# Scan pass of a two-layer image model: rows by channel then state, replicated in a quarter of the transfers; gathered rows squared in thirds; compare marks in 8 bits; a ring of six tie masks

## What is computed

```python
sim = jnp.einsum('bdl,bd->bl', xn, cn)
sort_idx = jnp.argsort(-sim, axis=1)
inv_idx = jnp.argsort(sort_idx, axis=1)
xseq = jnp.take_along_axis(x_conv.reshape(b, D, L), sort_idx[:, None, :], axis=2)
xs = jnp.stack([xseq, jnp.flip(xseq, -1)], axis=1)
...
def step(hst, t):
    dt_l, B_l, C_l, x_l = t
    dA = jnp.exp(dt_l[..., None] * A)
    hst = dA * hst + (dt_l * x_l)[..., None] * B_l[:, :, None, :]
    y = jnp.einsum('bkdn,bkn->bkd', hst, C_l)
    return (hst, y)
...
y = jnp.take_along_axis(y, inv_idx[:, None, :], axis=2).reshape(b, D, h, w)
yl = jnp.transpose(y, (0, 2, 3, 1))
mu = jnp.mean(yl, -1, keepdims=True)
var = jnp.var(yl, -1, keepdims=True)
yl = (yl - mu) / jnp.sqrt(var + 1e-05) * norm_gamma + norm_beta
```

## Time and profile before

| | |
|---|---|
| median of three runs | 18248.87 us |
| the profiled execution | 18395.5 us |
| its span, first to last instruction | 18392.4 us |
| a lap of pass one, mean of ten | 307.9 us |
| pass one | about the first 10300 us of the span |
| PE, DVE, ACT, POOL busy, of the span | 72%, 77%, 48%, 67% |
| mean granted TensorE clock | 0.826 of full speed |

### The profile page before, as it was taken

How to read it: one execution, slowest core, us unless ns; L and a number is a source line. 1 busy time by engine, 2 the same in 40 slices (tenths; PEclk the granted TensorE clock), 3 DMA queues, 4 the chain that set the end, 5 groups by cost and what they waited for, 6 DMA issues and landing times. The chain is left out here.

```text
span 18392.4 us, 187064 instructions
## 1 busy us (share of the span) xinstructions
PE 13268.3 (72%) x52714; PEld 6518.8 (35%) x53295; DVE 14108.2 (77%) x18932; ACT 8908.6 (48%) x16476; POOL 12335.6 (67%) x10756
## 2 busy tenths in 40 slices
PE   6777777777777777777776366666666666666665
PEld 3333333333334333433332133333333333333332
DVE  4788888888878888888877277777777777777777
ACT  4556565655555555555554244444444444444442
POOL 3777777777777777777777266666666666666665
PEclk8899999999999999999988577777777777777776
DMA  2333333333333333333333355555555555555554
GB/s 53 96 99 99 98 99 97 101 96 100 96 95 101 97 101 97 101 97 100 98 95 94 88 159 160 158 157 157 154 159 159 158 160 160 161 158 155 158 159 130
DMA packets 1297950, 2235.15 MB, mean 122 GB/s; under 512 B 713341, under 2 KB 759125, under 8 KB 1284629
## 3 DMA queue, kind: packets, MB, share of 16 engines
q1 hardware_dynamic: 896022, 1090.20, 22.8%
q0 software_dynamic: 368640, 1076.24, 20.6%
q10 hardware_dynamic: 32256, 56.64, 1.0%
HBM read 1493.27 MB, written 275.76 MB: 96 GB/s over the span
## 5 line engine op out<-in xcount | busy, mean ns | idle before, releaser
L1608 POOL DMA_INDIRECT G<-corners,idx x5184 | 4929.0, 951 | 3260.6 <-issue 1407.9
L1368 POOL TENSOR_TENSOR hc<-h,crep 128x768 f32<-128x768 f32 x2304 | 4177.3, 1815 | 2245.5 <-DVE h L1165 1086.8
L1149 DVE TENSOR_TENSOR ps<-dxr,ps 128x768 f32<-128x768 f32 x2304 | 2192.2, 951 | 1274.4 <-PE ps L752 1103.9
L1165 DVE TENSOR_TENSOR_SCAN h<-decay,carry,ps 128x768 f32<-128x768 f32 x1536 | 2777.0, 1808 | 90.6 <-ACT decay L986 37.5
L763 PE MATMUL ps<-hc,sel 128*96 128x512 f32 (+1 forms) x6144 | 2431.7, 521 | 474.9 <-POOL hc L1368 362.7
L986 ACT ACTIVATE decay<-dtr,a_neg 128x768 f32<-128x768 f32 x2304 | 2121.5, 927 | 522.3 <-DVE h L1165 504.4
L1897 DVE TENSOR_TENSOR G<-G,ps 128x1152 f32<-128x1152 f32 (+1 forms) x1152 | 1724.8, 1497 | 0.0
L1639 PE MATMUL ps<-cols_t,w_def 128*96 128x384 f32 x3456 | 1443.5, 583 | 316.2 <-ACT prow L1827 298.9
L752 PE MATMUL ps<-bq,pick 128*128 128x256 bf16 (+1 forms) x4027 | 1083.8, 342 | 795.3 <-DVE h L1165 496.2
L763 PEld LDWEIGHTS ps<-hc,sel 128*96 128x96 f32 x6144 | 972.7, 174 | 1678.5 <-issue 1058.8
L883 PE MATMUL ps<-xcp,w_local 128*96 128x384 f32 x3456 | 1459.0, 544 | 130.3 <-ACT local_c L1054 130.3
(11 more groups left out here) (235 smaller groups left out, 24443.8 us busy)
## 6 DMA issues: line engine op xcount, KB each, us to landing
crep<-c_rows SPq DMA_DIRECT2D x3072, 96.0 KB
dtr<-rel SPq DMA_DIRECT2D x2304, 96.0 KB
dxr<-one_e SPq DMA_DIRECT2D x2304, 96.0 KB
corners<-prow SPq DMA_DIRECT2D x1536, 72.0 KB
G<-corners,idx POOLq DMA_INDIRECT x5184
x_in<-in_x SPq DMA_DIRECT2D x32, 864.0 KB
local_all<-local_c ACTq DMA_DIRECT2D x192, 144.0 KB
sim<-sorted_rows SPq DMA_DIRECT2D x32, 864.0 KB, 6.8
```

The lines of the kernel that those rows point to most:

```text
L1149: dve.tensor_tensor(drive, dxr[:, q % 2, cg, :], drive, ALU.mult).then_inc(S["s_drive"], 1)
L1165: dve.tensor_tensor_scan(along(h[:, v % HR, :], k), along(decay[:, v % 3, :], k), along(wide(bank_of("step", v % STEPS), P), k), first, AL ...
L1368: pool.tensor_tensor(hc[:, v % HC, :], h[:, v % HR, :], crep[:, g % CRING, :], ALU.mult).then_inc(S["s_weighted"], 1)
L1608: pool.indirect_dma_start(M["G"][:, slot(g), k, :], None, table(r), bass.IndirectOffsetOnAxis(M["idx"][side(r)][:, t, k:k + 1], 0)).then_i ...
```

## The change

1. **Rows by channel, then state.** Row `p` of the 128 becomes channel `p // 4` of state `p % 4`. The constants `pick` and `sel` and the load of `a_log` follow; so a replication is one transfer to 128 rows whose source repeats each row four times, three instead of 12 for `dtr` and for `dxr`, one instead of four for `crep`. All bytes are moved as before.
2. **Gathered rows squared in thirds.** ACT squares six tiles each in steps 13, 16 and 19, each tile with an accumulated sum, and waits only for the six gathers that it needs (a semaphore for each third). DVE's sum of the squares goes; the roots are made in steps 20 and 21, the scaling in 22 to 24.
3. **Comparisons** start at step 17 instead of 19, in 8 bits; the tie masks start at 16, a step ahead of the comparisons, in a ring of six.
4. `HC` is six. The normalisation starts at step 38 instead of 40, and a chunk's nine taps are spread over four steps (3, 2, 2, 2) from step 44. The first round's state inputs come in step 4 instead of 3.

```diff
-    state = np.repeat(np.arange(N).reshape(NG, NG), GS, axis=1)
+    state = np.tile(np.arange(N).reshape(NG, NG), (1, GS))
...
-    c["sel"] = (np.arange(P)[:, None, None] % GS + GS * np.arange(CG)[None, :, None] == r[None, None, :]).astype(
+    c["sel"] = (np.arange(P)[:, None, None] // NG + GS * np.arange(CG)[None, :, None] == r[None, None, :]).astype(
...
-HC = 5
+HC = 6
...
-E_NORM = 17
+E_SQUARE = (13, 16, 19)
+E_NORM = 20
...
-O_CMP = 19
+O_CMP = 17
+O_TIE = O_CMP - 1
+TIES = 6
...
-NORM = 40
+NORM = 38
 CONV = NORM + 6
+CONV_TAPS = (0, 3, 5, 7, TAPS)
+CPARTS = len(CONV_TAPS) - 1
...
-BC_AT = (3, 16, 27, 38, 51, 63)
+BC_AT = (4, 16, 27, 38, 51, 63)
...
                 for g in range(CG):
-                    for j in range(NG):
-                        sp.dma_start(rep[j * GS:(j + 1) * GS, q % 2, g, :],
-                                     src[g * GS:(g + 1) * GS, :]).then_inc(S[f"{done}{g}"], 16)
+                    sp.dma_start(rep[:, q % 2, g, :], src[g * GS:(g + 1) * GS, :].unsqueeze(1).to_broadcast([GS, NG, SC])
+                                 ).then_inc(S[f"{done}{g}"], 16)
...
-                for j in range(NG):
-                    n = NG * (g % NG) + j
-                    sp.dma_start(crep[j * GS:(j + 1) * GS, g % CRING, :],
-                                 dram["c"][q % 2, n:n + 1, :].partition_broadcast(GS)).then_inc(S[f"s_crep{g % CRING}"], 16)
+                n = NG * (g % NG)
+                sp.dma_start(crep[:, g % CRING, :], dram["c"][q % 2, n:n + NG, :].unsqueeze(0).to_broadcast([GS, NG, SC])
+                             ).then_inc(S[f"s_crep{g % CRING}"], 16)
...
-                    for t in range(3 * part, 3 * part + 3):
+                    for t in range(CONV_TAPS[part], CONV_TAPS[part + 1]):
...
+                if s in E_SQUARE:
+                    i = E_SQUARE.index(s)
+                    act.wait_ge(S[f"e_gather{i}"], (lap[0] + 1) * each_gather)
...
+                    for t in range(TPS * i, TPS * (i + 1)):
+                        m = act.activation(M["e_squares"][:, t % TPS, :], ended[:, t, :], ACT.Square,
+                                           accum_out=M["var_y"][:, t:t + 1])
+                    m.then_inc(S["e_sq"], 1)
                 n = s - E_NORM
                 if n == 0:
-                    act.wait_ge(S["e_gather"], past("e_gather") + 16 * NT)
...
-                    act.activation(e_squares, ended[:], ACT.Square).then_inc(S["e_sq"], 1)
...
                 if n == 1:
-                    dve.wait_ge(S["e_sq"], past("e_sq") + 1)
-                    dve.tensor_reduce(var_y[:], e_squares, AX.X, ALU.add).then_inc(S["e_var"], 1)
-                if n == 3:
...
-                t, _ = sub_chunk(s, O_CMP, 1, NT)
+                t, _ = sub_chunk(s, O_TIE, 1, NT)
...
-                    if t >= 2:
-                        pool.wait_ge(S["o_ranked"], past("o_ranked") + t - 1)
+                    if t >= TIES:
+                        pool.wait_ge(S["o_ranked"], past("o_ranked") + t - TIES + 1)
```

More of the change, by code:

```diff
@@ L272, in build_program @@
                      "s_added", "s_y", "s_yturned", "s_yrows", "s_ystored",
[L273 to L274 removed]
+                     *[f"e_gather{i}" for i in range(NSC)], "e_sq", "e_root", "e_inv", "e_norm", "e_back", "e_out", "e_saved0", "e_saved1")
+            dma = [S["o_scatter"], *[S[f"e_gather{i}"] for i in range(NSC)]]
             own = [s for s in S.values() if s not in dma]
@@ L476, in pass_one_memory @@
         tall=tall, x=low("x_in", [L]), xn=b("xnp", [P, PH, PW]), xpad=low("xcp", [PH, PW]), sim=b("sim", [P, L]),
-        rows=b("rows", [P, NT, C]), unit=b("unit", [P, NT, C]), cmp=b("cmp", [P, 2, L], BF16),
-        tie=b("tie", [P, 2, P], BF16), same=b("same", [P, P]), one=b("one", [P, 1], BF16), work=low("work", [3, CH]), local=b("local_c", [C, 2, CH]),
+        rows=b("rows", [P, NT, C]), unit=b("unit", [P, NT, C]), cmp=b("cmp", [P, 2, L], FP8),
+        tie=b("tie", [P, TIES, P], BF16), same=b("same", [P, P]), one=b("one", [P, 1], BF16),
+        one8=b("one8", [P, 1], FP8), e_squares=b("e_squares", [P, NT // NSC, C], BF16), work=low("work", [3, CH]), local=b("local_c", [C, 2, CH]),
         zpart=b("zpart", [C, NCH]), rlen=b("rlen", [P, NT]), root_x=b("root_x", [P, NT]), dist=b("dist", [P, NT]),
@@ L513, in pass_one, with gathered @@
     dtr, dxr, crep, decay, h, hc = (M[n] for n in ("dtr", "dxr", "crep", "decay", "h", "hc"))
+    each_gather = 16 * NT // NSC
+    def gathered(eng, laps_done):
+        for i in range(NSC):
+            eng.wait_ge(S[f"e_gather{i}"], laps_done * each_gather)
     chunk = lambda c: slice(c * CH, (c + 1) * CH)
@@ L650, in store_rows @@
                 if E and i == 1:
-                    sp.wait_ge(S["e_gather"], past("e_gather") + 16 * NT)
+                    gathered(sp, lap[0] + 1)
                 tiles = slice(TPS * c, TPS * (c + 1))
@@ L1019, in normalise @@
                     act.activation(newton, inv, ACT.Square).then_inc(S["n_inv"], 1)
-                c, part = sub_chunk(s, CONV, 3)
-                if c is not None and part == 2:
+                c, part = sub_chunk(s, CONV, CPARTS)
+                if c is not None and part == CPARTS - 1:
                     act.wait_ge(S["n_conv"], past("n_conv") + c + 1)
@@ L1075, in end @@
                     act.activation(M["sq_y"][:], M["inv_y"][:], ACT.Square).then_inc(S["e_root"], 1)
-                if 4 <= n < 4 + NSC:
+                if 2 <= n < 2 + NSC:
                     act.wait_ge(S["e_inv"], past("e_inv") + 1)
-                    for t in range(TPS * (n - 4), TPS * (n - 3)):
+                    for t in range(TPS * (n - 2), TPS * (n - 1)):
                         m = act.activation(ended[:, t, :], ended[:, t, :], ACT.Copy, scale=M["root_y"][:, t:t + 1])
@@ L1224, in order @@
                     if j == 0 and E:
-                        dve.wait_ge(S["e_gather"], past("e_gather") + 16 * NT)
+                        gathered(dve, lap[0] + 1)
                     if j == 0 and lap[0]:
@@ L1333, in ties @@
                     pool.wait_ge(S["o_same"], past("o_same") + t + 1)
-                    pool.tensor_tensor(M["tie"][:, t % 2, :], M["same"][:], Wt["before"][:],
+                    pool.tensor_tensor(M["tie"][:, t % TIES, :], M["same"][:], Wt["before"][:],
                                        ALU.mult).then_inc(S["o_tie"], 1)
             def pad(s):
-                c, part = sub_chunk(s, CONV + 3, 3)
+                c, part = sub_chunk(s, CONV + CPARTS, CPARTS)
                 if c is not None and part == 0:
@@ L1384, in _ @@
             if E:
-                pool.wait_ge(S["e_gather"], laps * 16 * NT)
+                gathered(pool, laps)
             if O:
```

50 lines of the change are left out of this document (24 added, 26 removed).

## The result

| | before | after |
|---|---|---|
| median of four runs | 18250.65 us | 18093.13 us |
| the profiled execution, and its span | 18395.5, 18392.4 us | 18102.84, 18101.0 us |
| ten laps of pass one | 3079.0 us | 3017.0 us |

The ratio is 0.991, with an interval of 0.9894 to 0.9926. The change is faster by about 160 us, where 579 were forecast and the range ended at 240. The two profiled executions stand 292.7 us apart, more than the medians; of that, 131 us lie behind the last lap, in pass two, which the change does not touch. So I go by laps, 6.2 us shorter in these ten instead of 18.7.

A forecast was written before the change was run, and what follows sets the result against it. A pass-one lap is DVE's work plus its idle time, with POOL or DVE full by stretch. 8.2 - 1 + 1 + 4 + 5.5 + 1 = 18.7 us a lap, 579 in all, gave 17670 us (17400 to 18010).

The forecast's parts named there:

- The first state inputs in step 4: Moving them puts 1.6 us of POOL's work behind the first `rel`, in the same stretch: forecast to cost nothing.
- Spreads: Merged `dtr` and `dxr` transfers: gains of 1 us a lap at the first `dxr` and 4 in the fifth round.
- The issues shrink from 7.6 to 1.9 us, less 1.1 for data: Fifth round, ACT's wait for `dxr` before overwriting `one_e`: 4.6 of 5.64 us saved, taken as 4 (1 to 4.8).
- the term of 1 us: DVE's 3.7 us wait for the first `dxr` ends, but POOL bounds that stretch: 1 us a lap (0 to 3.7).
- Squares: DVE's sum and the wait before it go: 8.2 us a lap, not less than 4; ACT's price loses 1 (0 to 5).
- Masks: Masks made two POOL steps ahead of PE's use shorten DVE's waits for `replicate`: 5.5 us a lap (1 to 8).
- Taps: Same 54 taps a lap over 24 steps instead of 18, with HC and normalisation: gain of 1 us (-2 to 3).
- Eight bits: 8-bit comparison results on DVE, and PE's products with them: no time gained, only memory.
- POOL eats it: Rival, 0.17: DVE runs into POOL's products in both full stretches; 267 us gained, 17980; sign: PE's wait well above 11.6 us.
- The data, not the issues: Rival, 0.10: data set the spreads' length, so both spread terms vanish; 13.7 us a lap, 422 us gained, 17825.
- a merged transfer goes to so few DMA engines that it ends slower: Rival, 0.05: on four of 16 engines, third group 10 us late in each of six rounds; 19700 us.

The follow-up runs named there:

- the three moves: Changed kernel with comparisons at step 19 (masks at 18), first state inputs in step 3 and squares in steps 15, 17, 19: 0.9798 of the kernel before.
- the kernel of the squares: Kernel before with only the squares in thirds and 8-bit comparisons: 0.9916; with its comparisons and masks at step 17 instead of 19: 0.997.

## Why the prediction was wrong

**The account.** Worked out from ratios: squares 153 us, masks 97 to 119, spreads 55 to 62, taps 0; against it the state inputs in step 4, 66, and the comparisons at 17, 88 to 99. The sum lies between 140 and 180, and 157 to 172 were measured; such a sum takes it that the parts do not act on each other. The squares' steps do not appear in it: their cost shows only once the inputs are moved.

**The step that failed most** is "The first state inputs in step 4 ... nothing, the same work lies in the same stretch", together with the comparisons' start, for which my sum has no term at all. I counted work and not places, and POOL's work alone. PE's work is the same, but two insertions in one step leave no step between them and the `replicate`, and the bank that it needs is emptied behind the other insertion. The order of instructions showed both; I did not follow who frees the bank. In the same way the comparisons' two steps cost no instruction, yet they move the comparisons, their masks and POOL's scatters against a softplus and step sizes that stay where they were, and in steps 33 and 34 a `replicate` then stands behind a late mask. Together these are 154 to 165 us of the 420 that are missing; of the rest some 97 are the spreads (155 less 58), 63 the squares (216 less 153), 62 the masks (170 less 108) and 30 the taps. (My sum for the last lap, 8.2, left out the spreads and ACT's loss, which it has too: 12.2, a slip of 4 us.)

**Spreads**: the step "The issues shrink from 7.6 to 1.9 us, less 1.1 for data". The mechanism was right and the size wrong. SP's queue in the fifth round of the lap, and the wait that it ends, against the earlier trace rows:

```profile
3846.29 3.81 SPq L631 DMA_DIRECT2D dtr<-rel  x3
3850.14 5.70 SPq L631 DMA_DIRECT2D dxr<-one_e  x3
```

```profile
L948 ACT ACTIVATE one_e<-mag,ones 96x768 f32<-96x768 f32 x60 | 56.1, 935 | 48.8 <-DMA dxr<-one_e 47.2
```

Three transfers hold SP for 3.8 to 5.7 us, not 1.9. I had set the data of one group (1.5 us) against the issues of three; three groups are 1.18 MB, by my own 258 GB/s 4.6 us. (That the third transfer cannot be issued before the first has drained, as I put it for a later run, is not what the trace shows: the third `dtr` was issued by 3850.1, and the first landed at 3851.8.) The wait of ACT fell from 5.86 us a lap (58.6 in the ten laps of before) to 4.72, DVE's behind it from 4.27 to 2.44. The first `dxr` was in time in after, but that was luck. With the state inputs in step 4, POOL's `remainder_low` (L1317, 1.64 us) stands between its step sizes and its step inputs, and SP starts on `dxr` 5.1 us behind `dtr`. With the inputs back in step 3 it starts 3.9 us behind, and DVE waits 2.5 us again (2.8 in the three moves, where the old spreads make it 3.8): the first group lands 8.0 us after POOL had it ready, where I had worked out 4.4 without the `dtr` ahead of it in the queue. So the term of 1 us came out near its size, but not for the reason given. In after itself DVE waits for `replicate` in its stead, and steps 10 to 13 went from 17.7 to 18.4 us. Both terms together are worth 1.8 to 2 us a lap instead of 5. The Trainium skill says in "DMA: Bandwidth & Descriptors", section "Issuing engines are not separate DMA queues", that initiating is usually small beside the DMA; by it these terms were nothing, and the truth lies between its nothing and my 5.

**Squares**: 5.1 us a lap for 7.2. I had named what would be late next (POOL, whose gathers end where they ended) and the bound (4), and took the upper end nevertheless. In step 18 it was POOL's product that PE stood for, and not yet a mask. ACT's price was off too: each square is 267 ns and its sum another 186, 0.45 in all, within the bounds of 0.36 and 0.72.

```profile
L1083 ACT ACTIVATE e_squares<-unit 128x96 bf16<-128x96 f32 x180 | 48.0, 267 | 25.8 <-DMA unit<-scan_rows,rank 25.8
...
L1083 ACT ACTIVATION_READ_ACCUMULATOR e_squares<-unit 128x1 f32 x180 | 33.5, 186 | 0.0
```

**Masks**: 3.2 to 3.9 us a lap for 5.5, inside the bounds of 1 to 8. PE's wait for them fell to 11.0 a lap and not below 5. **Taps**: nothing for 1; the steps that I thought they would lengthen (the last ones) became shorter, and steps 39 to 48 longer by as much. **Eight bits**: nothing on DVE (1466 ns for 1468), as forecast.

**The rivals.** "POOL eats it" gave 17980, the nearest, but its mark is absent: PE's wait for POOL's product fell, from 11.6 to 8.9 us a lap. In steps 31 to 38 it is true all the same: there POOL is busy 34.4 of 36.3 us before and 32.6 of 35.8 after. "The data, not the issues" holds for two thirds of the spreads. That a merged transfer goes to so few DMA engines that it ends slower is excluded: while SP issued the six transfers above, from 3846.3 to 3855.9, the 16 engines were busy 0.83 of the time, more than 12 of them on average, where that rival needed fewer than seven.

**What is left open**: in the changed kernel the cost of the comparisons at 17 lies in steps 33 and 34, behind the masks. In the kernel of the squares, which has two mask places, it is spread over steps 31 to 38, and the 60 us or so apart from the standstill were not traced to one instruction there. `HC` of six and the 8-bit comparisons had no run of their own.

## What to carry to other kernels

Price an edit by what it stands behind afterwards: an instruction that is moved at equal work costs what the buffers, banks and in-order queues around its new place make the next one wait, so follow for each who frees what it needs. A bundle of edits can be worth less than half of its good parts; undoing them one at a time, and adding the ratios, found 200 us more than the whole had given. When transfers are merged, compare the issues saved with the data of all of them that share the queue, not of one.

## What the runs showed of the hardware

A DVE instruction on SBUF can stand still while POOL multiplies two SBUF operands: 0.95 us became 3.0 in step 37, with two operands, and 0.55 became 2.6 with one; the accumulating form with one operand kept its 0.94. Nothing in the profile names this as a wait; it shows as a longer instruction. Behind the scan, whoever was first went through: where DVE was, it kept 0.93 us and the product took 2.44 instead of 1.82; where the product was, DVE took up to 2.58. The Trainium skill states it in "SBUF — State Buffer", section "Who interferes with whom": a DVE instruction with two SBUF inputs contends with a GpSimd one that reads SBUF, one in a two-port mode with GpSimd in general, whoever issues first holds the other off, and the form of `tensor_scalar` that writes out its accumulator does not enter such a mode. These traces agree, by the numbers above; that the plain scaling ran in a two-port mode is not shown by them. My sum did not apply the rule to an instruction that the change leaves alone. One row asks more: in step 37 DVE began 0.35 us before the product and stood all the same, while a scatter of POOL was still running.
